# Four-layer graph network on one core: GpSimd's 800 row scatters of the sorted edge table, in batches with waits for their landing

## What is computed

```
edge_index = jnp.stack([src, dst])
h = relu(layernorm(x)); x = x + L0(h, src, dst, ...)          # attention over the edges
h = relu(layernorm(x)); x = x + L1(h, edge_index, ...)        # two Chebyshev convolutions
h = relu(layernorm(x)); x = x + L2(h, edge_attr_64, ...)      # messages with edge features
h = relu(layernorm(x)); x = x + L3(h, ..., src, dst)          # attention over the edges

def L2(node_feats, edge_feats, ..., edge_index):
    message = relu(node_feats[edge_index[1]] + edge_feats)            # gathered by dst
    message_reduce = segment_sum(message, edge_index[0], num_nodes)   # summed by src
    h = (1.0 + eps) * node_feats + message_reduce
    return relu(layernorm(h @ W1 + b1) * ln_g + ln_b) @ W2 + b2
```

## Time and profile before

| | |
|---|---|
| device time, 3 runs | 2887.59 us median (2884.13 to 2894.74) |
| span of the profiled execution | 4076.3 us |
| POOL busy in it | 1592.5 us (39%), 1665 instructions |
| DVE busy | 2238.4 us (55%) |
| PE busy | 1936.6 us (48%) |
| the scatters, L1229 | 800, 792.0 us busy, 990 ns each, 736.3 us of idle time ahead of them |
| bytes moved by all queues | 266.91 MB, 65 GB/s over the span |

### The profile page before, as it was taken

One profiled execution on the slowest core, in us unless ns is written; L12 is line 12 of the kernel. 1 busy time (PEld: TensorE's weight loads), 2 busy tenths in 40 slices (PEclk: granted clock), 3 DMA queues, 4 the chain that ended last, 5 costly groups with the idle time before them and its releaser, 6 DMA issues. The chain is left out here.

```text
span 4076.3 us, 62411 instructions
## 1 busy us (share of the span) xinstructions
PE 1936.6 (48%) x16923; PEld 1342.4 (33%) x16923; DVE 2238.4 (55%) x4872; ACT 1209.9 (30%) x3818; POOL 1592.5 (39%) x1665
## 2 busy tenths in 40 slices
PE   5835544454444444330223249992211255655377
PEld 4623333333333333220111126661111245545222
DVE  6876766666676776430211013323211399997899
ACT  1154444444444444230001002100000133334744
POOL 0055555555555555456766640006667400000000
PEclk8966666666666666665555569995555598896599
DMA  8611111111111111542222210004443222221000
GB/s 277 249 42 40 40 40 40 40 40 40 40 40 40 40 40 40 172 124 55 59 52 53 52 34 1 0 11 138 136 115 102 61 75 83 74 82 42 0 0 8
DMA packets 399312, 266.91 MB, mean 65 GB/s; under 512 B 321473, under 2 KB 349310, under 8 KB 399090
## 3 DMA queue, kind: packets, MB, share of 16 engines
q1 hardware_dynamic: 306278, 87.81, 10.1%
q10 hardware_dynamic: 41488, 118.96, 8.1%
q0 software_dynamic: 51488, 59.40, 6.0%
HBM read 158.59 MB, written 107.47 MB: 65 GB/s over the span
## 5 line engine op out<-in xcount | busy, mean ns | idle before, releaser
L1229 POOL DMA_INDIRECT sorted_edges<-r_load,r_to x800 | 792.0, 990 | 736.3 <-DMA r_to<-places 439.6
L805 POOL DMA_INDIRECT hsrc<-h,edges x808 | 778.4, 963 | 693.5 <-PE ps L998 460.1
L873 DVE TENSOR_TENSOR prod<-ps,hsrc 125x1024 f32<-125x1024 f32 x200 | 245.0, 1225 | 323.3 <-remote 180.1
L996 PE MATMUL ps<-blank 128*64 128x160 bf16 x101 | 31.5, 312 | 590.2 <-remote 579.3
L1401 PE MATMUL ps<-R,w_work 128*128 128x64 bf16 x3000 | 145.1, 206 | 272.3 <-DVE R L1743 148.2
L1537 ACT ACTIVATE R<-w_work 128x384 bf16<-128x384 f32 (+1 forms) x160 | 85.8, 536 | 617.6 <-DVE w_work L1733 506.5
L1733 DVE TENSOR_TENSOR w_work<-ps,w_work 128x384 f32<-128x384 f32 (+1 forms) x160 | 91.2, 570 | 306.3 <-remote 296.6
L1391 PE MATMUL ps<-R 128*128 128x64 bf16 x3000 | 142.9, 208 | 225.5 <-issue 132.7
L1331 PE MATMUL ps<-R,A 128*128 128x192 bf16 x1250 | 183.0, 267 | 138.8 <-issue 136.0
L864 DVE TENSOR_SCALAR hot<-ramp,small 125x400 bf16<-125x400 int16 x800 | 219.6, 326 | 49.9 <-issue 47.7
L952 ACT ACTIVATE lo<-ramp,edges 125x128 bf16<-125x128 int16 x808 | 246.8, 387 | 0.0
(11 more groups left out here) (414 smaller groups left out, 4419.4 us busy)
## 6 DMA issues: line engine op xcount, KB each, us to landing
w_work<-sorted_edges ACTq DMA_DIRECT2D x42, 1000.0 KB
sorted_edges<-A ACTq DMA_DIRECT2D x25, 1000.0 KB, 7.3
r_load<-in_edge_attr_dram SPq DMA_DIRECT2D x80, 312.5 KB
dstrow<-dst_rows SPq DMA_DIRECT2D x101, 234.4 KB
counts<-A ACTq DMA_DIRECT2D x5, 4000.0 KB, 30.2
A<-counts SPq DMA_DIRECT2D x12, 1600.0 KB
sorted_edges<-A ACTq DMA_DIRECT2D x3, 5000.0 KB, 28.7
hsrc<-h,edges POOLq DMA_INDIRECT x808
```

What stands on the lines that cost most here:

```text
L805: g.indirect_dma_start(out=hsrc[:, s, t, :], out_offset=None, in_=S.h0[:, :], in_offset=bass.IndirectOffsetOnAxis(ap=edges.bitcast(I32)[:, ...
L873: v.tensor_tensor(prod[0:TP, :].rearrange("p (t h f) -> p t h f", t=HT, h=H), S.ps[0:TP, hf * 1024:(hf + 1) * 1024].rearrange("p (t h f) - ...
L1229: g.indirect_dma_start(out=S.sorted, out_offset=bass.IndirectOffsetOnAxis(ap=to[:, hf, t:t + 1], axis=0), in_=load[:, hf, t, :], in_offset ...
```

## The change

Inside each half the ten scatters are cut into batches of 4, 3 and 3. Ahead of the scatters `t` = 4 and `t` = 7 GpSimd waits until all scatters of this half so far have landed, and behind the tenth it waits once more. Each wait is followed by an increment of a semaphore that nobody waits for (`carrier`). There are three new waits for each half, 240 in all; no instruction that moves data is added, removed or moved, and SP's, ScalarE's, VectorE's and TensorE's code is the same as before.

```
     AFTER = 23
+    BATCH = (4, 7)
     TAKE = 2
...
                     for t in range(HALF):
+                        if t in BATCH:
+                            g.wait_ge(qr[f"sc{hf}"], c * (16 * HALF) + 16 * t)
+                            g.sem_inc(qr["carrier"], 1)
                         g.indirect_dma_start(out=S.sorted, out_offset=bass.IndirectOffsetOnAxis(ap=to[:, hf, t:t + 1], axis=0),
                                              in_=load[:, hf, t, :], in_offset=None).then_inc(qr[f"sc{hf}"], 16)
+                    g.wait_ge(qr[f"sc{hf}"], c * (16 * HALF) + 16 * HALF)
+                    g.sem_inc(qr["carrier"], 1)
```

## The result

The changed kernel takes 3370.95 us (median of 4 runs, 3369.08 to 3372.81), and the kernel before takes 2889.88 us beside it on the same chip. The ratio is 1.1671 with a 95% interval of 1.1654 to 1.1688: 481 us, or 17%, slower. The forecast was 3250 us with a range of 3100 to 3390.

The account below looks back on a forecast made before the run. It took `spread` as 1185 us, its message loop's end set by VectorE with scatters some 75 us ahead. Waits add 78 x 6.0 = 468 us; less cover +394, settled at +365: 3252, rounded 3250 us, range 3100 to 3390.

Parts of the forecast that it names:

- What the extra 1189 us are: Profiled 4076.3 us against the timed median 2887.6: engines slow beside indirect DMAs, read as a cost of being recorded.
- rebuilt execution: Timed execution pieced together from profile parts, without slow stretches: `mlp` and `gat` 378 us, `spread` taken as 1185.
- The base chain: GpSimd's scatters in `spread` before the change: 66 us, then 78 halves at 12.95, in sum 1076 us.
- The cover: Message loop: scatters run some 75 us ahead of its end, so that much of the 468 us added is hidden.
- One wait, +2.0 us: Gap at a GpSimd wait: landing 1.1, restart 0.8, sharing with loads 0.4, 2.3 us, 2.0 more than today.
- The halved sharing, -28 us: Half of the 0.4 us load sharing per wait may be the recording's doing; settled +365 between +394 and +347.
- The profiled execution, about 4220 us: Profile span after the change: 4076 + 145, with SP's stand at L1203 shrinking from 347 to about 120 us.
- Rival 1: Cheap waits: landing never shares, each GpSimd wait costs 1.4 to 1.6 us more, time 3146 to 3188; chance 0.14.
- Rival 2: Scatters closer when timed: the 0.30 us gap is the recording's, a half 9.9 us, time 3114; chance 0.08.
- Rival 3: Dear waits: each GpSimd wait costs 3.3 us more, a half 22.85, time some 3590; chance 0.06.
- Rival 4: No change: `spread` is bound by its engines at 1270 us, waits cost at most 0.7 us more; chance 0.03.
- Rival 5: Faster: engines beside scatters are really slow and waits relieve them, at most 100 us, down to 2790; chance 0.04.

Follow-up runs that it names:

- e4_before_again: The kernel before, unchanged, profiled and timed again on the second sort of chip: 4088.09 us, with a span of 4086.4.
- e5_first24: The changed kernel with its three waits in chunks 0 to 23 alone, first sort: 3147.99 us, ratio to the kernel before 1.0893.
- e6_last16: The changed kernel with its three waits in chunks 24 to 39 alone, first sort: 3109.66 us, ratio to the kernel before 1.0745.
- e3_landed_already: The kernel before plus 234 waits, each for the other half's rows, issued at least four scatters earlier; second sort: 4080.95 us, ratio 0.9979.
- e7_wait_each: The changed kernel with a wait behind each of the ten scatters of a half, first sort: 4538.40 us, ratio to the kernel before 1.5705.
- e2_inner_only: The changed kernel without the wait behind the tenth scatter, two inner waits kept, second sort: 3678.13 us, ratio to the kernel before 0.8987.
- e12_landed_already_third: Called the base: the kernel before plus 234 waits for the other half's earlier-issued rows, as in e3_landed_already, on the first sort: 2887.09 us, ratio 0.9986.

## Why the prediction was right, and where it was wrong

The direction and the mechanism hold on the sort of chip on which it was timed: the waits lengthen GpSimd's chain, and the chain sets the loop's end. That GpSimd paces all 40 items is wrong, it paces the last 20; this cost nothing, since only the end counts. The result lies 121 us above the forecast, inside the range, and several steps were wrong and partly made up for each other.

**What the extra 1189 us are: wrong.** The prediction read the slow stretches as a cost of being recorded. `e4_before_again` and 4088 us in the timed executions show that it can take that long when timed. A span and a granted clock are on record for every timed execution on either sort, so recording is not what sets them apart; whether it plays any part in either was not isolated. The consequence was harmless by luck: that first layer, products and moves are fast in the executions timed here is what the rebuilt execution assumed. Its parts came out well: the first two stages end at 1327 (it put `front` and `attend` at some 1325), and the base's `spread` takes 2519 - 1327 = 1192 us against 1185.

**The base chain: 72 us too short.** The prediction put the last scatter 1076 us into the stage; it is 1148. It took 0.990 us for a scatter from the second sort; on the first sort it is 1.066 on average. That makes 853.1 us busy instead of 792.0, 61 of the 72 us; the rest is in the gaps.

**The cover: mis-sized, 75 us for 12.** It followed from the short chain (1111 us against the 1185 taken for the stage). With 1148 and some 43 us behind the last scatter (2475 to 2519) the scatters already nearly set the loop's end before the change, with the 13 us of cover read above. `e5_first24` and `e6_last16` settle this: were there 75 us of cover, or cover that depends on the place, the last column of the table would not read 10 to 14 throughout.

**One wait, +2.0 us: right as a sum, 493 / 240 = 2.05.** Its parts were not, and that they cancel is luck. The gap is 2.70 us rather than 2.3: the floor is 2.05 where landing and restart were put at 1.9 (no row shows the 0.6 us for SP's restart in that sum), and some 0.65 lie above it where the sharing with loads was put at 0.4. Against that, GpSimd's waits for SP's loads, which the prediction let stand, fell by 46 us (`DMA r_to<-places`, 56.6 us in the base and 10.3 after; 30 of them are the one stand near the start), and the scatters themselves by 27 us (853.1 to 825.8 busy). That the price is landing and restart and not the instruction is shown by `e3_landed_already` and its repeats.

**The halved sharing, -28 us: wrong.** It rested on the loads being stretched by recording. What was to be halved, the part of a gap above the floor, measured 0.65 us on a chip without the slow stretches, more than the 0.4 and not less.

**The sum.** Forecast: 468 - 75 - 28 = 365. Measured: 493 - 12 = 481. Of the 116 us between them, 63 are the cover, 28 the halved sharing, and 25 the chain's growth.

**The profiled execution, about 4220 us: wrong.** On the sort of chip of the profile before, the changed kernel spans 3765.8, so it falls by 310 us from the earlier trace rows where +145 was forecast. The slow stretches were taken to stay; they go. The stand at L1203 does not shrink to 120 us but is gone, and the idle time of the scatters is 844.5 us there (816.3 on the first sort), not 980, since 347 us came back rather than 227.

**The rivals.** Rival 1 (a wait for 1.4 to 1.6 us more) fails: even the floor in `e7_wait_each` is 1.75 more, and the chain grows by 1.9 at least. Rival 2 fails: the spacing is 1.27 us. Rival 3 fails as a mean; single gaps reach it. Rival 4 fails. Rival 5 has the right mechanism on the second sort of chip and nothing to act on in the first; the price put on it, 100 us, was far too low there (330 us, and 410 with two waits), because it was bounded by a timed execution in which the slow stretches are absent.

What stays open: what differs between the two sorts of chip; why GpSimd standing for a landing frees the other engines (a pause of the same length without a landing was not tried); and what two waits for a half cost on the first sort, where `e2_inner_only` was not run (on the second it is the fastest of the three). No variant beats the kernel before there, and one wait costs 4.9% there while it gives 9% on the other.

## What to carry to other kernels

A wait for the landing of an indirect DMA of 40 KB costs the issuing engine some 1.75 us at least, and 2.2 (`e7_wait_each`) to 2.4 (the changed kernel) on average, over the 0.3 us between two that follow each other freely; before putting it in, look how far that engine's chain already is from the stage's end, since each microsecond beyond that is paid in full. When a profile is far longer than the timed median, don't explain it away: run the same kernel again and see whether timed executions can be that long, because here the two came from different sorts. And when two kernels are compared in the same stretch of time, look whether it holds the same work in both. A change that thins a stream of indirect DMAs has to be timed on both sorts, and the sign of one doesn't carry to the other.

## What the runs showed of the hardware that was not expected

- The same kernel takes 2889 us on some chips and 4088 us on others, and keeps to one of them through a whole set of runs. The difference lies in the stretches with indirect DMAs: the first layer takes 1110 or 1476 us, the products 539 or 1059; the last two stages take 370 us in `e12_landed_already_third` and 378 in the earlier trace rows. In the slow first layer a register move on SP takes 0.69 us at the median instead of 29 ns.
- On the slow sort, the stretch from the first scatter to the last sum of the fourth product shrinks from 1042 us to 869, 664 and 569 with no, one, two and three waits for each ten scatters; the 84 casts of the transposes in it from 211 to 80, 67 and 67.
- From start to landing a scatter of 40 KB takes 2.2 us at the median and 7.2 at most. The gap behind a wait is 2.03 to 2.08 us where nothing disturbs it (566 of 799 in `e7_wait_each`).
- The mean duration of the same scatter instruction was 0.983 us in `e7_wait_each`, 1.032 in the changed kernel and 1.066 in the base on the first sort, with the median at 0.967 to 0.969 in all three; single ones take up to 2.5 us. There the mean grows with the density of the stream; on the second sort it is 0.990 us with no wait at all. The cause was not isolated.
